# Batch 0's early heads two tiles sooner, the peak rows ahead of the stacks, and stacks in runs of 2 KB: one edit at the seam between a gated convolution and a cross-attention

## The reference, cut to what matters

```python
# x: (8, 256, 512), ctx: (8, 256, 128), all float32
def conv_block(x):                        # D_INNER = 1024, 4 taps, depthwise and causal
    xi, gate = split(x @ w_in.T)
    h = silu(conv(xi) + conv_b) * D * silu(gate)
    return h @ w_out.T
def cross(q, ctx):                        # 16 heads of 32, causal
    qp = q @ Wq.T;  k, v = split(ctx @ Wkv.T)
    scores = where(causal, qh @ kh.T / sqrt(32), -big)
    return (softmax(scores) @ vh) @ Wout.T
x = layernorm(x + conv_block(x))
x = layernorm(x + cross(x, ctx))
x = layernorm(x + shared_ffn(x) + top2_of_8_experts(x))
```

## Time and profile before

| | |
|---|---|
| median of 3 runs | 1041.78 us (1041.15 to 1044.91) |
| the profiled execution | 1046.52 us, span 1044.9 us, mean granted clock 0.974 |
| PE busy | 978.4 us, 94% of the span |
| DVE, ACT, POOL busy | 65%, 51%, 26% |
| convolution | 0 to about 302.6 us |
| cross-attention | about 302.9 to 528 us |

### The profile page before, as it was taken

The page is one execution under the profiler, slowest core; times in us unless marked ns, Lnnn a source line. Parts: engine busy times, 40 slices in busy tenths (PEclk is TensorE's granted clock), DMA queues, the critical chain, the costliest instruction groups (busy, mean ns, idle before and its releaser), DMA issues. The chain is left out here.

```text
span 1044.9 us, 17392 instructions
## 1 busy us (share of the span) xinstructions
PE 978.4 (94%) x5776; PEld 833.6 (80%) x5776; DVE 678.8 (65%) x1556; ACT 528.9 (51%) x1262; POOL 267.8 (26%) x388
## 2 busy tenths in 40 slices
PE   7899999999967999998889979999999999999996
PEld 5688888888757888887667768999898988778785
DVE  4837646378256788887557747777767765254576
ACT  5523404235366898889743246566656654221120
POOL 4610020102523333333431022222222220603040
PEclk9999999999987899999899999999999999899999
DMA  4503004021747899987541268778877882705042
GB/s 162 201 2 121 0 29 182 0 81 61 222 108 174 269 246 259 254 234 206 186 158 40 84 204 263 263 248 276 276 245 249 274 260 72 240 23 197 4 166 76
DMA packets 85647, 172.75 MB, mean 165 GB/s; under 512 B 8624, under 2 KB 33712, under 8 KB 83792
## 3 DMA queue, kind: packets, MB, share of 16 engines
q1 hardware_dynamic: 76928, 146.54, 44.7%
q0 software_dynamic: 8080, 24.91, 7.5%
q10 hardware_dynamic: 576, 0.52, 0.2%
HBM read 131.05 MB, written 37.49 MB: 161 GB/s over the span
## 5 line engine op out<-in xcount | busy, mean ns | idle before, releaser
L45 PE MATMUL a_ps_proj<-region_a_rounded,arena 128*128 128x512 f32 x272 | 107.8, 396 | 10.1 <-DVE region_a_rounded L459 6.2
L45 PE MATMUL e_ps_h<-e_x_lo,e_gu_hi 128*128 128x256 f32 (+1 forms) x384 | 110.8, 289 | 2.8 <-DVE e_x_lo L2216 1.3
L46 PE MATMUL e_ps_h<-e_x_hi,e_gu_lo 128*128 128x256 f32 (+1 forms) x384 | 107.5, 280 | 0.0
L47 PE MATMUL e_ps_h<-e_x_hi,e_gu_hi 128*128 128x256 f32 (+1 forms) x384 | 107.5, 280 | 0.0
L46 PE MATMUL a_ps_proj<-region_a_rounded,arena 128*128 128x512 f32 x272 | 106.9, 393 | 0.0
L47 PE MATMUL a_ps_proj<-region_a_rounded,arena 128*128 128x512 f32 x272 | 106.8, 393 | 0.0
L141 ACT ACTIVATE b_dump<-b_dump,b_peak 128x128 f32<-128x128 f32 x232 | 102.7, 446 | 5.5 <-DVE b_peak L133 5.4
L478 DVE SCALAR_TENSOR_TENSOR f_region_b<-a_ps_proj,a_taps,f_region_b 128x510 f32<-128x510 f32 (+2 forms) x96 | 71.6, 746 | 41.3 <-ACT f_region_b L408 39.1
L2222 DVE TENSOR_TENSOR e_gu_lo<-f_region_a,e_gu_hi 128x704 fp32r<-128x704 f32 x92 | 81.2, 886 | 17.3 <-ACT e_gu_hi L2128 16.7
L133 DVE CUSTOM_DVE_ANT_0 b_dump<-b_ps_s,b_mask 128x128 f32<-128x128 f32 x232 | 72.7, 352 | 24.7 <-PE b_ps_s L127 24.2
L2128 ACT ACTIVATE e_gu_hi<-f_region_a 128x704 fp32r<-128x704 f32 x92 | 71.8, 785 | 25.5 <-PEq L1532 15.1
(11 more groups left out here) (415 smaller groups left out, 2702.0 us busy)
## 6 DMA issues: line engine op xcount, KB each, us to landing
f_region_a<-we_gate_up SPq DMA_DIRECT2D x88, 352.0 KB, 5.4
qk_split<-arena SPq DMA_DIRECT2D x24, 512.0 KB, 6.0
y_slots<-f_region_b SPq DMA_DIRECT2D x16, 512.0 KB, 4.5
f_x_next<-x SPq DMA_DIRECT2D x6, 1024.0 KB, 7.6
b_sk<-qk_split SPq DMA_DIRECT2D x24, 256.0 KB, 4.6
f_region_a<-we_down SPq DMA_DIRECT2D x12, 512.0 KB, 4.4
f_region_b<-we_down SPq DMA_DIRECT2D x11, 512.0 KB, 4.1
b_sq<-qk_split SPq DMA_DIRECT2D x21, 256.0 KB, 5.9
```

The source lines that it names most:

```text
L45: pe.matmul(out, a_hi, b_lo, start=first, stop=False)
L46: pe.matmul(out, a_lo, b_hi, start=False, stop=False)
L47: return pe.matmul(out, a_hi, b_hi, start=False, stop=last)
```

## The change

Four things are edited.

1. PE's twelve early scores begin two output tiles sooner: behind tiles 18 to 29 of 32 instead of 20 to 31. DVE adds the residual for the first tile behind the eleventh head and for the other three behind all maxima.
2. Where the stacks come from is laid out so that each run of the transfers has 2 KB instead of 1 KB. A half of the stack holds its 8 heads as (h, c) instead of (c, h), so that a partition's two chunks c are adjacent; the high and low tiles in SBUF hold (batch, chunk, token) instead of (chunk, token of both batches). The bytes moved and the partitions stay as they are. `attend` reads its weights through `slot_of`, and waits for 7, 8, 15 and 16 cut heads before its four chunks instead of 4, 8, 12 and 16.
3. Batch 1's first half of the stacks goes from SP alone; SP then waits for the two peak rows (`m_loaded`) before it issues the second half. POOL issues the rows first.
4. At the start of the cross-attention PE does two scores before the value products, ACT and DVE do their peaks first and round the transposed rows after the last sums and the shift.

The diff, cut to its core:

```diff
-        first_sq, first_sk = (r[:, 0:8 * GT].rearrange("p (c h t) -> p c h t", c=DC, h=HC) for r in rounded)
+        first_sq, first_sk = (r[:, 0:8 * GT].rearrange("p (u h n) -> p u h n", u=2, h=HC) for r in rounded)
...
-                queue.dma_start(stack[r * HD:(r + 1) * HD, :, h].bitcast(F32), tile[h * HD:(h + 1) * HD, :, 0:S].bitcast(F32))\
+                queue.dma_start(stack[r * HD:(r + 1) * HD, :, h].bitcast(F32),
+                                tile[h * HD:(h + 1) * HD, 0].rearrange("p (u c) t -> p u (c t)", u=2).bitcast(F32))\
                     .then_inc(done, 16)
...
-                    sp.dma_start(split_dram[1, u, kind].rearrange("p (c t) -> p c t", c=DC // 2).bitcast(F32),
-                                 tile[:, 2 * u:2 * u + 2, S:2 * S].bitcast(F32)).then_inc(ahead_stored, 16)
+                    sp.dma_start(split_dram[1, u, kind].bitcast(F32),
+                                 tile[:, 1, 2 * u:2 * u + 2].rearrange("p c t -> p (c t)").bitcast(F32)).then_inc(ahead_stored, 16)
...
             for n in range(EARLY):
                 maxima(n)
-                if n >= EARLY - TILES:
-                    add_x(LAST, x1, [n - (EARLY - TILES)])
                 if n == EARLY - 2:
                     dve.wait_ge(log_done, 1)
                     soft.lower(dve, 0).then_inc(soft.shift_done, 1)
+                    add_x(LAST, x1, [0])
+            add_x(LAST, x1, [1, 2, 3])
...
-                        if j >= scored:
-                            score((j - scored) * TILES + t)
+                        if scored <= j * TILES + t < scored + EARLY:
+                            score(j * TILES + t - scored)
...
-            output(LAST, BEFORE, JC, JC - EARLY // TILES)
+            output(LAST, BEFORE, JC, JC * TILES - EARLY - 2)
...
+        def slot_of(c, h):
+            return UH * (c // UC) + UC * h + c % UC
...
-                queue.dma_start(into[b % 2][r * HD:(r + 1) * HD, u].rearrange("p (c h) t -> p c h t", c=UC).bitcast(F32),
-                                split_dram[b % 2, u, s].rearrange("(h r) (c t) -> r c h t", h=HC, c=UC).bitcast(F32))\
+                queue.dma_start(into[b % 2][r * HD:(r + 1) * HD, u].rearrange("p (h c) t -> p h (c t)", c=UC).bitcast(F32),
+                                split_dram[b % 2, u, s].rearrange("(h r) n -> r h n", h=HC).bitcast(F32))\
                     .then_inc(loaded, 16)
...
-            stack(sp, sk, 1, 0, (KH, KL, KH), stack_loaded[0])
+            load_stack(1, 0)
+            sp.wait_ge(m_loaded, 32 * half_count(0, 0))
             load_stack(1, 1)
...
-            stack(pool, sq, 1, 0, (QL, QH, QH), pool_moved)
             load_peaks(0, 0)
...
-            totals(0, 1, EARLY - UH)
             peaks(0, 0)
+            totals(0, 1, EARLY - UH)
             totals(0, 1, EARLY - UH + 1)
             context(GB)
-            turned(GB, 0)
-            turned(GB, 1)
             for i in range(EARLY - UH + 2, UH):
                 totals(0, 1, i)
             logs(0, 1)
+            turned(GB, 0)
+            turned(GB, 1)
...
-            values(0, 1)
-            maxima(0, 1, EARLY - UH)
             peaks(0, 0)
-            values(0, 0)
-            for i in range(EARLY - UH + 1, UH):
+            for i in range(EARLY - UH, UH):
                 maxima(0, 1, i)
-                if i == UH - 2:
-                    turned(GB, 0)
-                    turned(GB, 1)
+                if i >= UH - 2:
+                    values(0, UH - 1 - i)
             shifts(0, 1)
+            turned(GB, 0)
+            turned(GB, 1)
...
-                    pe.wait_ge(cut_done, HEADS * b + HC * (c + 1))
+                    pe.wait_ge(cut_done, HEADS * b + slot_of(c, HC - 1) + 1)
```

More of the change, by code:

```diff
@@ L227, in gated_conv, with ahead_bank @@
         following = cross.units
-        k_hi, k_lo, q_hi = (arena[:, (5 + k) * DC * D:(6 + k) * DC * D].rearrange("p (c t) -> p c t", c=DC)
+        k_hi, k_lo, q_hi = (arena[:, (5 + k) * DC * D:(6 + k) * DC * D].rearrange("p (b c t) -> p b c t", b=GB, c=DC)
                             for k in range(3))
-        q_lo = x_raw[:].bitcast(F32R)
+        q_lo = x_raw[:].bitcast(F32R).rearrange("p c t -> p (c t)").rearrange("p (b c t) -> p b c t", b=GB, c=DC)
         AHEAD = [(kind, c) for kind in ("x", "k", "q") for c in range(DC)]
         BEFORE = 2
-        def ahead_bank(n):
-            return ps_proj[:, n // 2 % 2, n % 2]
+        def ahead_bank(n, kind="x"):
+            bank = ps_proj[:, n // 2 % 2, n % 2]
+            return bank if kind == "x" else bank.rearrange("p (b t) -> p b t", b=GB)
         def ahead_hi(kind, c):
-            return {"k": k_hi, "x": x_hi, "q": q_hi}[kind][:, c]
+            return x_hi[:, c] if kind == "x" else {"k": k_hi, "q": q_hi}[kind][:, :, c]
         def ahead_lo(kind, c):
-            return {"k": k_lo, "x": x_lo, "q": q_lo}[kind][:, c]
+            return x_lo[:, c] if kind == "x" else {"k": k_lo, "q": q_lo}[kind][:, :, c]
         def stack_ahead(queue, stack, r, tile, done):
             for h in range(HC):
-                queue.dma_start(stack[r * HD:(r + 1) * HD, :, h].bitcast(F32), tile[h * HD:(h + 1) * HD, :, 0:S].bitcast(F32))\
+                queue.dma_start(stack[r * HD:(r + 1) * HD, :, h].bitcast(F32),
+                                tile[h * HD:(h + 1) * HD, 0].rearrange("p (u c) t -> p u (c t)", u=2).bitcast(F32))\
                     .then_inc(done, 16)
@@ L366, in _ @@
                 for u in range(2):
-                    pool.dma_start(split_dram[1, u, kind].rearrange("p (c t) -> p c t", c=DC // 2).bitcast(F32),
-                                   tile[:, 2 * u:2 * u + 2, S:2 * S].bitcast(F32)).then_inc(pool_moved, 16)
+                    pool.dma_start(split_dram[1, u, kind].bitcast(F32),
+                                   tile[:, 1, 2 * u:2 * u + 2].rearrange("p c t -> p (c t)").bitcast(F32)).then_inc(pool_moved, 16)
             pool.memset(rounded[1][K_ROWS:M_ROWS].bitcast(F32), 1.0)
@@ L437, in _ @@
                 act.wait_ge(ahead_ready, n + 1)
-                act.activation(ahead_hi(kind, c), ahead_bank(n), ACT.Copy).then_inc(ahead_hi_done, 1)
+                act.activation(ahead_hi(kind, c), ahead_bank(n, kind), ACT.Copy).then_inc(ahead_hi_done, 1)
                 if n in (DC - 1, DC):
@@ L513, in _ @@
                 dve.wait_ge(ahead_hi_done, 1 + n + 1)
-                dve.tensor_tensor(ahead_lo(kind, c), ahead_bank(n), ahead_hi(kind, c).bitcast(F32), ALU.subtract)\
+                dve.tensor_tensor(ahead_lo(kind, c), ahead_bank(n, kind), ahead_hi(kind, c).bitcast(F32), ALU.subtract)\
                     .then_inc(ahead_lo_done, 1)
@@ L553, in score, with output @@
                 soft.score(pe, ps_proj[:, 1, n % 2], q, k).then_inc(s_ready, 1)
-            def output(g, first, end, scored=JC):
+            def output(g, first, end, scored=JC * TILES):
                 pe.wait_ge(w_lo_done, W_UNITS)
@@ L742, in stack_count @@
         def stack_count(b, u):
-            return 96 * b - 48 * (1 - u)
+            return 96 * b
         def stack(queue, into, b, u, parts, loaded):
             for r, s in enumerate(parts):
-                queue.dma_start(into[b % 2][r * HD:(r + 1) * HD, u].rearrange("p (c h) t -> p c h t", c=UC).bitcast(F32),
-                                split_dram[b % 2, u, s].rearrange("(h r) (c t) -> r c h t", h=HC, c=UC).bitcast(F32))\
+                queue.dma_start(into[b % 2][r * HD:(r + 1) * HD, u].rearrange("p (h c) t -> p h (c t)", c=UC).bitcast(F32),
+                                split_dram[b % 2, u, s].rearrange("(h r) n -> r h n", h=HC).bitcast(F32))\
                     .then_inc(loaded, 16)
@@ L932, in attended @@
                     .then_inc(a_hi_done, 1)
+            peaks(0, 0)
             totals(0, 1, EARLY - UH)
-            peaks(0, 0)
             totals(0, 1, EARLY - UH + 1)
             context(GB)
-            turned(GB, 0)
-            turned(GB, 1)
             for i in range(EARLY - UH + 2, UH):
@@ L1202, in scores @@
                     pe.wait_ge(stack_loaded[u], stack_count(b, u))
-                    if b == 1 and u == 0:
-                        pe.wait_ge(pool_moved, 16 * (2 * HC + 4 + 3))
                 if n >= 2:
@@ L1246, in attend @@
                             mm = pe.matmul(ps_o[h * HD:(h + 1) * HD, c // UC, c % UC * S + r * P:(c % UC + 1) * S],
-                                           v[:, b % 2, r, head * HD:(head + 1) * HD], pt[:, head, 2 * r * P:(2 + r) * P],
+                                           v[:, b % 2, r, head * HD:(head + 1) * HD],
+                                           pt[:, slot_of(c, h), 2 * r * P:(2 + r) * P],
                                            start=r == 0, stop=r == BT - 1)
@@ L1292, in _ @@
             peaks(0, 0)
+            scores(0, 1, EARLY - UH)
+            scores(0, 1, EARLY - UH + 1)
             value(0, 1)
-            scores(0, 1, EARLY - UH)
             value(0, 0)
-            for i in range(EARLY - UH + 1, UH):
```

(1 more changed line is left out.)

## The result

| | before | changed |
|---|---|---|
| median, us (20 runs each, side by side) | 1044.44 | 1039.29 |
| lowest and highest, us | 1041.03, 1048.43 | 1035.68, 1042.55 |
| ratio of the times, 95% interval | | 0.995 [0.9937, 0.9963] |
| profiled execution: span, mean clock | 1044.9 us, 0.974 | 1034.9 us, 0.982 |

The change saves 0.5%, 5.2 us (3.9 to 6.6). The forecast had 5.3 us and 1036.5 us; the measured time is 2.8 us above that, since the kernel before took 1044.44 us over 20 runs and not the 1041.78 us of the three shown, from which the forecast started. The two profiled executions differ by 10.0 us, twice as much as the medians: one execution may not be read as the change.

A forecast was written before the change was run, and what follows sets the result against it. PE, busy 94% of the span, was taken as the bound, with gains only at the seam before attention. 4.5 + 0.25 + 1.0 less 0.4, say 5.3 us, took 1041.78 to 1036.5 us, range 1031.0 to 1041.6.

The forecast's parts named there:

- The rows and the held half: Start of batch 1's attention: rows ahead of the stacks, half the stacks behind them, start the loop 4.5 us sooner.
- The first half lands at S + 8.5: Batch 1's stacks: SP's first six transfers were to land 8.5 us after the attention block's start.
- The rows I had at S + 9.0: Peak rows on POOL's queue: 6.3 us from issue to landing, so in 9.0 us after the block's start.
- The new wait on SP: SP before batch 1's second half: waiting for the rows costs nothing, since its first score comes eight heads later.
- Runs of 2 KB: Stack transfers: no gain from DRAM or in steady batches; early stacks from SBUF 1.0 us sooner, between 0 and 3.8.
- Two tiles sooner: Convolution's end: early scores moved ahead of two tiles mostly move idle time; this part alone gains 0.25 us.
- the clock, for which I had 0.4: Behind the early scores' longer wait: 0.4 us lost to the lower granted clock.
- The sum: Whole kernel: 4.5 + 0.25 + 1.0, less 0.4 for the clock, say 5.3 us saved, giving 1036.5 us.
- Rival 1: Stack transfers: 2 KB runs raise 32 partitions to 385 GB/s, early stacks 2.5 us sooner; 1031.4 us, chance 0.13.
- Rival 2: Peak rows still land late, 10.8 us after the block's start; 1.8 us less gain, 1038.3 us, chance 0.14.
- Rival 3: First attention batch swallows the gain as ACT's exponentials and sums bunch up; 3 us less, 1039.5 us, chance 0.09.
- Rival 4: Clock stays low after the early scores' wait and at the loop's start; slower, 1044.0 us, chance 0.09.

The follow-up runs named there:

- e12: The changed kernel run again unaltered, to see the spread between executions: 1038.98 us, ratio 0.9957 to the kernel before.
- e10: Changed kernel with the two tiles and the runs of 2 KB undone, leaving the rows' order and held second half: 1039.28 us, ratio 0.9959 to before.
- e7: Changed kernel with the old order of PE, ACT and DVE at the attention's start, rows written late, transfers as changed: 1039.72 us, ratio 0.9955 to before.
- e6: Changed kernel without the hold on SP, POOL issuing the first half's three query transfers ahead of the rows: 1042.89 us, ratio 0.9971 to before.
- e9: Changed kernel with both the old engine order and the old transfer issue at the attention's start: 1042.53 us, ratio 0.998 to before.
- e5: Changed kernel, but SP issues all twelve stack transfers without waiting for the peak rows: 1037.99 us, ratio 0.9934 to before.
- e4: Transfers alone, no computation, runs of 1 against 2 KB: from DRAM 221 and 227 GB/s into 32 partitions, 278 and 343 into 128.
- e2: Changed kernel with the old layout, runs of 1 KB in stack transfers and batch 1's stores: 1040.67 us, ratio 0.9978 to before.
- e3: Changed kernel, but PE waits for the early stacks in four parts, one head pair at a time: 1038.43 us, ratio 0.994 to before.
- e1: Changed kernel with early scores back behind tiles 20 to 31 and additions between the last maxima: 1038.85 us, ratio 0.9958 to before.
- e8: Changed kernel with early stacks awaited in four parts and early scores back behind tiles 20 to 31: 1036.94 us, ratio 0.9908 to before.
- e11: The kernel of e8 run a second time, beside the changed kernel: 1038.36 us, ratio 0.9944 to before.

## Why the prediction was right

**The rows and the held half: 4.5 us forecast, 3.8 and 4.0 measured** (S + 13.46 to S + 9.66, and to S + 9.42 in e12). This term is the change: e10, which has it alone, saves as much as all of it within 2 us. Two steps were off. "The first half lands at S + 8.5" was short by 0.5 us, and that is what PE waits for; and the score of 0.6 us that PE does between this landing and the first `below_peak` was not counted. The rows I had at S + 9.0 were in by S + 8.2. The reason given for the gain was in part the wrong one. I wrote that the rows come sooner because POOL issues them sooner with nothing of its own ahead. e7 shows that the sooner issue is worth nothing once the second half is held and POOL has no stacks ahead; e6 that these are worth 0.9 us once the rows are issued soon; and e9 that undoing both costs 2.8. The rest of the 3.8 (13.46 against 12.42 in e9) goes with what else e9 has, the runs of 2 KB or the two tiles: SP issues the nine transfers in 4.4 us in e9 and took 6.2 before. But this is one order of counting: e10, with runs of 1 KB and the tiles as before, has all but 0.2 us of the 3.8.

**The new wait on SP** costs nothing, as forecast, and e5 shows that it also brings little: 0.8 us at the loop's start, nothing in the time.

**Runs of 2 KB: from DRAM nothing, early stacks 1.0 us forecast.** The first is right (e4: 221 and 227 GB/s), the second wrong: up to gate is 27.14 us against 27.16, and SP still takes a median of 1.39 us to issue one of the eight transfers. The slow issue that I took for the queue's is not cured by fewer, longer runs; e4 has no difference there either. SP's issues of the early stacks in the changed kernel (min/median/max in ns), answering to the earlier trace rows:

```profile
L246 SPq DMA_DIRECT2D region_b_rounded<-arena x8: 592/1388/1803, 266.9 to 275.5; - x8
```

What I did not count is that the issue of a DRAM stack falls by 0.2 us, with which six of them land up to 0.9 us sooner (first scores at S + 8.8 to 9.3 in the seven profiles with the hold and 2 KB, against S + 9.3 and 9.8 in e10 and e2). Whether this reaches the time stays open: e2 is 0.3% above the changed kernel, e10 level with it.

**Two tiles sooner: 0.25 us forecast; 1.2 us longer in the profile.** Three steps failed. The tail behind PE's last tile is S's wait, 1.85 us against 2.90 before, so it shrank by 1.05 us while PE's work behind the gate grew by 1.38: 0.3 us lost. I had it shrink by as much as the work grew. DVE's three additions in a row, which I let end just before ACT, end last. The other 0.9 us is the clock, for which I had 0.4: it stays at 0.50 for 5.07 us (6.16 in e12) instead of 3.41. I put this down to the longer wait, and that is not shown. Of the eight profiles with the tiles moved, five have a slow stretch of 5 to 6.4 us behind waits of 3.79 to 4.42 us (changed, e12, e5, e6, e9), but e2, e7 and e3 have one of about 3.4 us behind 4.34, 3.87 and 2.22 us, and lose only 0.35 us from gate to S against before. What sets its length stays open. The block's start, which was to come 0.5 to 2 us sooner, came 1.2 us later counted from "up". In the time the part is nil within 2 us (e1 0.9958, changed 0.995).

**The sum.** Up to attend the profiles give -4.6 and -2.8 us (e12), the medians -5.2 and, by e12's ratio, -4.5 with an interval of 2.2 to 6.8. The forecast's 5.3 was 1.25 us of gains that no run shows, less 0.4, and a main term too large by 0.5 to 0.7. That it still fell within 0.2 us of the 5.2 measured is in part luck. What makes up for the difference is not located; in the first profile it is the shorter batch (2.0 us), of which 1.4 is the spread between executions (e12), and two profiles that differ by 1.8 us up to attend for one and the same kernel can't show more.

**The rivals.** Rival 1 (runs count) falls as it was priced, at 385 GB/s and early stacks 2.5 us sooner, by e4 and by the gate in e2; that the runs are worth something smaller stays open. Rival 2 had the rows land at S + 10.8; they land by S + 8.2, though e6 and e9 show that its mechanism exists with the full backlog (8.0 and 7.3 us). Rival 3 (swallowed in the first batch) would have shown as a longer batch; it is 0.6 to 2.0 us shorter. Rival 4 saw the clock's cost at the gate, about 0.9 us in the changed kernel's profile and 1.3 in e12's where it had 1.6, but none beyond the price before in e2 and e7; and the batch behind it, from loop to attend, had a mean clock of 0.81 and 0.75 in the two profiles and no more time than before.

## What to carry to other kernels

The small transfer that many wait for was late here only when two things met: it was issued late, and the whole of the stacks was already in hand. Removing either cured most of the delay. Undo each alone, and then both together, before you say which of the two paid: of two cures for one delay each looks worth little when it is undone alone. A thing that is used sooner must also arrive sooner: here the stacks, not PE's place in its list, set the first score, and moving the scores up turned work into a wait. And where two executions of one kernel differ by 8 us in their span, as e12's and the first did (1043.1 and 1034.9), one profile tells which wait ends last, and only a series of runs tells what that is worth.

## What the runs showed of the hardware

- Into 32 partitions fewer, longer runs made the issue cheaper, not the transfer: 0.66 to 0.47 us of SP for 256 KB from DRAM, at 221 and 227 GB/s. Into 128 partitions the same step gave 278 to 343 GB/s.
- From 32 partitions of SBUF to 32 others, 192 GB/s in runs of 1 KB and 201 in runs of 2 KB, and an issue of 0.65 us for half the bytes.
- Two transfers of 8 KB on POOL's queue, issued 1.5 us after S, land 4.0 to 4.4 us after their issue with six stacks in runs of 1 KB on SP's queue (e2, e10) and 5.1 to 6.9 with the same bytes in runs of 2 KB (changed, e12, e1, e3, e8, e11). Issued at S + 4.4 beside the latter they need 4.1 to 4.3 (e7). With nine stacks on SP's queue and three ahead of them on POOL's own they need 7.1 to 8.5 (e9, e6, before); with all twelve on SP's, 5.0 to 6.7 (e5).
- The granted clock fell to 0.52 behind the wait of 2.77 us of the kernel before and to half behind 1.95 us (e11), and stayed at 1.00 behind 2.79 us in e10, with the same order of instructions on PE around it in all three. The wait's length alone does not say whether it falls. Nor does it say how long it stays down: about 3.4 us behind waits of 1.95 to 4.34 us in six profiles (before, e1, e2, e3, e7, e11), 5 to 6.4 us behind 3.79 to 4.42 us in five.
